# A fused stack of four graph layers: probabilities of the second graph turned through DRAM and VectorE

## What is computed

```python
# layer 0: attention with 4 heads
Wh = (x @ W).reshape(B, N, H, F)
e = leaky_relu(e_src[:, :, None, :] + e_dst[:, None, :, :], 0.2)
alpha = softmax(where(adj > 0, e, NEG_INF), axis=2)
x = layernorm(x + elu(einsum('bijh,bjhf->bihf', alpha, Wh)))
# layer 1: three rounds of neighbour sum and GRU cell
for i in range(3):
    aggr = einsum('bst,bsd->btd', adj != 0, h @ weight[i])
    h = gru_cell(aggr, h)
x = layernorm(x + h)
# layer 2: per relation r = 1..4 of adj == r, sum and weight; adj holds 0 and 1 here
x = layernorm(x + sum_r (adj == r) @ x @ weight[r] + bias)
# layer 3: attention with one head
x = layernorm(x + elu(softmax(where(adj > 0, e3, NEG_INF)) @ (x @ W3.T)))
```

## Time and profile before

| what | us |
|---|---|
| median of 3 runs | 2617.78 (2617.44 to 2618.26) |
| span of the profiled execution | 2616.2 |
| TensorE busy in it | 2564.6 (98%) |
| VectorE busy | 2064.6 (79%) |
| ScalarE busy | 1629.9 (62%) |
| GpSimd busy | 1093.8 (42%) |
| mean granted TensorE clock | 0.992 of full |

### The profile page before, as it was taken

One profiled execution on the slowest core, in us unless ns is written; L12 is line 12 of the kernel. 1 busy time (PEld: TensorE's weight loads), 2 busy tenths in 40 slices (PEclk: granted clock), 3 DMA queues, 4 the chain that ended last, 5 costly groups with the idle time before them and its releaser, 6 DMA issues.

```text
span 2616.2 us, 48544 instructions
## 1 busy us (share of the span) xinstructions
PE 2564.6 (98%) x14979; PEld 2219.6 (85%) x14979; DVE 2064.6 (79%) x5210; ACT 1629.9 (62%) x4153; POOL 1093.8 (42%) x1264
## 2 busy tenths in 40 slices
...
DMA packets 265105, 128.99 MB, mean 49 GB/s; under 512 B 139760, under 2 KB 249840, under 8 KB 264816
## 3 DMA queue, kind: packets, MB, share of 16 engines
...
## 4 chain that ended last, share of the span: by engine, by line
PE 94%; DVE 1%; issue 1%; ACT 0%; POOL 0%; POOLq 0%; DVEq 0%; ACTq 0%
PE psum L938 60%; PE psum L792 10%; PE psum L926 6%; PE psum L853 6%; PE psum L975 3%; PE psum L842 3%; PE psum L869 2%; PE psum L811 1%; PE psum L913 1%; PE psum L861 1%; DVE stats L1351 0%; ACT x L1176 0%; POOL rstd L1508 0%; DVE first_scores L1322 0%; DVE moments L1355 0%
## 5 line engine op out<-in xcount | busy, mean ns | idle before, releaser
L938 PE MATMUL psum<-ag_h,wc_h 128*128 128x512 f32 (+1 forms) x1188 | 489.0, 412 | 2.7 <-issue 2.0
L938 PE MATMUL psum<-ht_h,whh_h 128*128 128x512 f32 (+1 forms) x1188 | 483.0, 407 | 0.7 <-ACT g_z L1159 0.6
L938 PE MATMUL psum<-ht_h,whh_l 128*128 128x512 f32 (+1 forms) x1188 | 462.8, 390 | 0.0
L938 PE MATMUL psum<-ag_l,wc_h 128*128 128x512 f32 (+1 forms) x1188 | 461.9, 389 | 0.0
L938 PE MATMUL psum<-ht_l,whh_h 128*128 128x512 f32 (+1 forms) x1188 | 461.7, 389 | 0.0
L938 PE MATMUL psum<-ag_h,wc_l 128*128 128x512 f32 (+1 forms) x1188 | 461.5, 388 | 0.0
L1506 POOL TENSOR_SCALAR rstd<-moments 128x2 f32<-128x2 f32 x256 | 73.3, 286 | 858.6 <-DVE moments L1355 854.1
L1557 POOL TENSOR_TENSOR ht<-ht,g_n 128x512 f32<-128x512 f32 (+1 forms) x198 | 251.7, 1271 | 71.3 <-ACT g_n L1164 63.7
L938 PEld LDWEIGHTS psum<-ht_h,whh_l 128*128 128x128 f32 x1188 | 224.9, 189 | 50.8
L938 PEld LDWEIGHTS psum<-ag_h,wc_l 128*128 128x128 f32 x1188 | 223.4, 188 | 50.5
L938 PEld LDWEIGHTS psum<-ht_l,whh_h 128*128 128x128 f32 x1188 | 225.7, 190 | 40.0
...
## 6 DMA issues: line engine op xcount, KB each, us to landing
first_scores<-first_kept SPq DMA_DIRECT2D x116, 256.0 KB, 3.7
adj_i<-in_adj_dram SPq DMA_DIRECT2D x128, 128.0 KB, 3.2
x_in<-in_x_dram SPq DMA_DIRECT2D x64, 256.0 KB, 3.8
out_dram<-out_t ACTq DMA_DIRECT2D x64, 256.0 KB, 2.5
x_blocks<-in_x_dram SPq DMA_DIRECT2D x464, 32.0 KB, 2.1
part<-in_adj_dram SPq DMA_DIRECT2D x32, 256.0 KB, 3.3
adj_g<-in_adj_dram SPq DMA_DIRECT2D x31, 256.0 KB, 3.3
last_scores<-last_kept SPq DMA_DIRECT2D x59, 128.0 KB, 3.0
```

What stands on the lines that cost most here:

```text
L938: last = mm(dst, s, m, start=(first and k == 0), stop=(last_part and k == len(flat) - 1))
```

## The change

For units from 6 on and the second graph of the unit (`scratched`), TensorE's four transposes and VectorE's copy go. In their place SP stores the unit's four probability tiles (256 KB) to a DRAM scratch (`pt_keep`), after ScalarE has made all eight, and loads them again in 32x32 pieces (`pt_blocks`, four DMAs of 64 KB) into a tile of the ring `xs`, and VectorE turns this with one block transpose of 128x512 into `first_turned`. The ring `xs` has three tiles instead of two, `wh` three. `x_blocks` is issued as four DMAs instead of eight. The scores tile of the second graph is free when it is stored. `att_pt(pre,1,0,1)` (now VectorE alone), `att_pv(pre,1,0)` and `att_exp(pre,1,0)` stand later in `HALF`. The weights of relations 2 to 4 aren't loaded at the start in one 768 KB tile, but one by one into a tile of 256 KB, by SP inside a branch like that of the other engines; SP reads the flag for it (`learn`).

```diff
-SLOTS = {"light": 4, "adj": 2, "x": 2, "xt": 1, "wh": 2,
+SLOTS = {"light": 4, "adj": 2, "x": 2, "xt": 1, "wh": 3,
...
-         "post_pen": 2, "post_t": 1, "post_pt": 1, "post_hn": 1, "post_y": 1, "x2s": 1, "h1": 1, "mt": 1, "adjt": 2, "x3": 2, "xs": 2,
+         "post_pen": 2, "post_t": 1, "post_pt": 1, "post_hn": 1, "post_y": 1, "x2s": 1, "h1": 1, "mt": 1, "adjt": 2, "x3": 2, "xs": 3,
...
+def scratched(kind, u, q):
+
+    return kind == "pre" and u >= BLOCKED and q == 1
...
+    if name == "att_pt" and not scratched(*a):
+        out.append("light")
...
-gru_r(0,0,0)  att_prob(pre,1,0)  rel_adjt(-2,1)
-gru_z(0,0,0)
+gru_r(0,0,0)  att_prob(pre,1,0)  pt_keep(1,0)  rel_adjt(-2,1)
+gru_z(0,0,0)  pt_blocks(1,0)
 gru_in(0,0,0)
-gru_hn(0,0,1)  att_pt(pre,1,0,0)  att_wh(post,-2,0,0)  gru_new(-1,1,1)  gru_split(-1,1)  att_pt(pre,1,0,1)
+gru_hn(0,0,1)  att_pt(pre,1,0,0)  att_wh(post,-2,0,0)  gru_new(-1,1,1)  gru_split(-1,1)
         att_wh(post,-2,0,1)  att_rows(post,-2,0)  att_spread(post,-2,0,0)  att_xt(pre,1,1)  rel_mask(-2,1)  gru_n(0,0,0)
-gru_rzh(0,0,1)  gru_turn(-1,1,0)  att_pv(pre,1,0)  gru_new(0,0,0)  att_wh(pre,1,1,0)  att_wh(pre,1,1,1)  att_rows(pre,1,1)
-        rel_h1(-2,1)  att_exp(pre,1,0)  gru_turn(-1,1,1)
+gru_rzh(0,0,1)  gru_turn(-1,1,0)  gru_new(0,0,0)  att_wh(pre,1,1,0)  att_wh(pre,1,1,1)  att_rows(pre,1,1)
+        rel_h1(-2,1)  gru_turn(-1,1,1)
 gru_r(0,0,1)  att_norm(post,-3,1)  rel_y1(-2,1)  att_spread(pre,1,1,0)  att_scores(post,-2,0,0)
-gru_z(0,0,1)  rel_rest(-2,1)
-gru_in(0,0,1)
+gru_z(0,0,1)  rel_rest(-2,1)  att_pt(pre,1,0,1)
+gru_in(0,0,1)  att_pv(pre,1,0)  att_exp(pre,1,0)
 gru_agg(-1,2,0)  att_prob(post,-2,0)  att_res(pre,1,0)  att_store(post,-3,1)  gru_n(0,0,1)  rel_norm(-2,1)
 gru_agg(-1,2,1)
 gru_hn(-1,2,0)  att_pt(post,-2,0,0)
 gru_rzh(-1,2,0)  att_xt(post,-2,1)  gru_new(0,0,1)  gru_split(0,0)  att_pv(post,-2,0)  att_spread(pre,1,1,1)
         att_scores(pre,1,1,0)  att_scores(pre,1,1,1)
 gru_r(-1,2,0)
-gru_z(-1,2,0)  att_wh(post,-2,1,0)  att_wh(post,-2,1,1)  att_exp(post,-2,0)  att_prob(pre,1,1)  x_blocks(2,0)  pre_load(2,0)
+gru_z(-1,2,0)  att_wh(post,-2,1,0)  att_wh(post,-2,1,1)  att_exp(post,-2,0)  att_prob(pre,1,1)  pt_keep(1,1)  x_blocks(2,0)  pre_load(2,0)
         gru_n(-1,2,0)
-gru_in(-1,2,0)
...
-        wrs = sb("wrs", [P, R - 1, C, D])
+        wr_other = sb("wr_other", [P, C, D])
...
+        pt_kept = [nc.dram_tensor(f"pt_kept{i}", (P, H0, P), F32, kind="Internal").ap() for i in range(2)]
...
+        TURNED = [s for s in order if s[0] == "att_xt" and blocked(*s[1:]) or s[0] == "att_pt" and scratched(*s[1:])]
...
+        def turned_on_pe(kind, u, q):
+
+            return min(u, BLOCKED) + u + q + 1 if kind == "pre" else u + 1
...
+                    (kind + "_t", "att_spread"): (s_pt_kept, 16 * (u - BLOCKED + 1)) if scratched(kind, u, q) else (L.pt_psum, turned_on_pe(kind, u, q)), (kind + "_pt", "att_pt"): (L.pv_psum, u + 1),
...
+            def pt_keep(u):
+                L = LAY["pre"]
+                sp.wait_ge(L.prob, 2 * L.heads * (u + 1))
+                if scratched("pre", u - 2, 1):
+                    sp.wait_ge(L.pt_ready, 2 * u - 2)
+                sp.dma_start(pt_kept[u % 2], L.scores[scores_slot("pre", u, 1)][:]).then_inc(s_pt_kept, 16)
+
+            def pt_blocks(u):
+                i = take(sp, "xs", "pt_blocks", u)
+                sp.wait_ge(s_pt_kept, 16 * (u - BLOCKED + 1))
+                blocks = pt_kept[u % 2].rearrange("(b i) h (a j) -> a i h b j", i=TURN, j=TURN)
+                for a in range(P // TURN):
+                    sp.dma_start(xs[i][a * TURN:(a + 1) * TURN].rearrange("i c n -> i (c n)").rearrange("i (h b j) -> i h b j", h=H0, j=TURN),
+                                 blocks[a]).then_inc(s_xs[i], 16)
+
             def x_blocks(u):
                 i = take(sp, "xs", "x_blocks", u)
-                blocks = x[2 * u:2 * u + 2].rearrange("g (b i) (c f j) -> c f i g b j", i=TURN, f=P // TURN, j=TURN)
-                for c in range(C):
-                    for g in range(P // TURN):
-                        sp.dma_start(xs[i][g * TURN:(g + 1) * TURN, c, :], blocks[c, g].rearrange("i g b j -> i (g b) j")).then_inc(s_xs[i], 16)
+                blocks = x[2 * u:2 * u + 2].rearrange("g (b i) (c f j) -> f i c g b j", i=TURN, f=P // TURN, j=TURN)
+                for f in range(P // TURN):
+                    sp.dma_start(xs[i][f * TURN:(f + 1) * TURN].rearrange("i c (m j) -> i c m j", j=TURN),
+                                 blocks[f].rearrange("i c g b j -> i c (g b) j")).then_inc(s_xs[i], 16)
 
             def gru_load(k):
...
-                sp.dma_start(wrs[:], L2_gnn_weight[1:R].rearrange("r (c p) o -> p r c o", p=P)).then_inc(s_rest, 16)
...
+            def rel_rest(u):
+
+                with sp.If(any_other > 0):
+                    for r in range(2, R + 1):
+                        after(sp, s_yr_ps, (R - 1) * u + r - 2)
+                        sp.dma_start(wr_other[:], L2_gnn_weight[r - 1].rearrange("(c p) o -> p c o", p=P)).then_inc(s_wr, 16)
+
...
+                if scratched(kind, u, q):
+                    return
...
-                if u == 0:
-                    pe.wait_ge(s_rest, 48)
...
+                        pe.wait_ge(s_wr, 16 * n)
...
-                                last = mm(LIGHT[:, i, q * D:(q + 1) * D], hr_t[:, c, q * P:(q + 1) * P], wrs[:, r - 2, c, :],
+                                last = mm(LIGHT[:, i, q * D:(q + 1) * D], hr_t[:, c, q * P:(q + 1) * P], wr_other[:, c, :],
...
-                    dve.wait_ge(s_xs[i], 128 * (rounds + 1))
+                    dve.wait_ge(s_xs[i], 64 * (rounds + 1))
...
-                L, i = LAY[kind], slot("light", "att_pt", kind, u, q)
+                L = LAY[kind]
                 pi = take(dve, kind + "_pt", "att_pt", kind, u, q)
-
                 dve.wait_ge(L.pt_ready, 2 * u + 1)
-                dve.wait_ge(L.pt_psum, 2 * u + q + 1)
-                nc.vector.tensor_copy(L.turned[pi][:].rearrange("p h n -> p (h n)"), LIGHT[:, i, :]).then_inc(L.pt_ready, 1)
+                turned = L.turned[pi][:].rearrange("p h n -> p (h n)")
+                if scratched(kind, u, q):
+                    i, rounds = ring("xs", "pt_blocks", u)
+                    dve.wait_ge(s_xs[i], 64 * (rounds + 1))
+                    nc.vector.transpose(turned, xs[i][:].rearrange("p c n -> p (c n)")).then_inc(s_xturned, 1)
+                    dve.wait_ge(s_xturned, TURNED.index(("att_pt", kind, u, q)) + 1)
+                    dve.sem_inc(L.pt_ready, 1)
+                else:
+                    i = slot("light", "att_pt", kind, u, q)
+                    dve.wait_ge(L.pt_psum, 2 * u + q + 1)
+                    nc.vector.tensor_copy(turned, LIGHT[:, i, :]).then_inc(L.pt_ready, 1)
```

More of the change, by code:

```diff
@@ L41 @@
     "pre_load": ("adj", "x", "pre_pen"), "post_load": ("adj", "post_pen", "adjf"),
-    "att_xt": ("xt",), "x_blocks": ("xs",), "att_direct": ("light",),
-    "att_pt": ("light",), "att_pv": ("light",),
+    "att_xt": ("xt",), "x_blocks": ("xs",), "pt_blocks": ("xs",), "att_direct": ("light",),
+    "att_pv": ("light",),
     "rel_adjt": ("light", "adjt"), "rel_bias": ("x2s",), "rel_mask": ("mt",),
@@ L108 @@
 gru_r(-1,2,0)
-gru_z(-1,2,0)  att_wh(post,-2,1,0)  att_wh(post,-2,1,1)  att_exp(post,-2,0)  att_prob(pre,1,1)  x_blocks(2,0)  pre_load(2,0)
+gru_z(-1,2,0)  att_wh(post,-2,1,0)  att_wh(post,-2,1,1)  att_exp(post,-2,0)  att_prob(pre,1,1)  pt_keep(1,1)  x_blocks(2,0)  pre_load(2,0)
         gru_n(-1,2,0)
-gru_in(-1,2,0)
+gru_in(-1,2,0)  pt_blocks(1,1)
 gru_hn(-1,2,1)  gru_turn(0,0,0)  gru_turn(0,0,1)  gru_load(1)
@@ L291, in placed @@
         return []
+    if name in ("pt_keep", "pt_blocks") and not scratched("pre", u, 1):
+        return []
     return [(name,) + kind + (u,) + a[2:]] if 0 <= u < 2 * halves - 2 else []
```

30 lines of the change are left out of this document (19 added, 11 removed).

## The result

The changed kernel takes 2973.99 us (median of 4 runs, 2971.48 to 2976.74) against 2618.02 us for the kernel before on the same chip: 1.136 times as long, interval 1.134 to 1.138. That is 356 us, or 12.3 us in each of the 29 rounds, where 8.6 were forecast. The time lies 4 us above the top of the range.

The account below looks back on a forecast made before the run. TensorE's matmul time was taken to set the span. Even unit 5.7, odd unit 1.7 and clock 1.2 made 8.6 us per round, x 29 = 249 us, giving 2867 us (+9.5%), range 2735 to 2970.

Parts of the forecast that it names:

- the chain at the even unit: Store waits for probabilities, adj_i queues behind it, GpSimd waits for adj_i, VectorE for GpSimd, TensorE for VectorE; 5.7 us net.
- the forecast signs: Changed kernel's profile: TensorE busy near 2539 us, 89%; waits near 2 and 6 us, 29 each; late adj_i; clock below 1.
- The even wait: TensorE at att_pv of the even unit waits 6.1 us for the turned tile; net of the saving +3.3 to +7.7.
- "by pieces" bound of 4.3: SP's four x block loads at the even unit take 4.3 us to issue if time goes by pieces; 2.7 was taken.
- The odd wait: TensorE waits 1.7 us at the odd unit, as VectorE's turn now stands behind the relation layer's statistics.
- 0.4 us added for SP's loads: Odd unit: SP's block loads ahead of the last layer's score rows may delay scores and VectorE; between 0 and 2.1 us.
- The saving: Four transposes per unit leave TensorE's stream, 0.44 us per unit, 25.5 us over 58 units.
- the term for the clock: TensorE's granted clock falls after a long wait, slowing the work behind it; 1.2 us per round, bounds 0 to 3.4.
- The third: Both units wait, block loads go by pieces, 6.8 us at low clock follows each wait; 2966 to 3039 us; chance 0.06.
- The second: Only the odd unit waits, slack absorbs the late even update; 2655 us; chance 0.08 with other partial waits.
- The fourth: Reloaded probabilities are themselves the late input, up to 2 us more per round, 2925 us; counted within the forecast's 0.80.
- The first: Everything is hidden, the engines keep ahead and only the 25.5 us go; 2592 us, faster; chance 0.04.

Follow-up runs that it names:

- e2_odd_turn: Changed kernel, but VectorE turns the odd unit's block right after rel_h1 instead of behind the relation layer's statistics; 2851.9 us, ratio 1.089.
- e3_filler: Changed kernel, with matmuls of unused result ahead of TensorE's waits for the turned tile, 7 at the odd unit, 20 at the even; 2841.86 us, ratio 1.086.
- e7_adj_first: Changed kernel, but at the even unit SP issues adj_i and x_in of the next unit ahead of the probability store; 2847.41 us, ratio 1.088.
- e1_sp_order: Changed kernel, but at the even unit SP stores and reloads the probabilities only after the next unit's loads are issued; 2749.27 us, ratio 1.048.
- the mended version: Changed kernel with SP's next loads first, odd turn right after rel_h1, even turned tile used after gru_hn(0,1,0); 2607.92 us, 0.997 of the kernel before.

## Why the prediction was off

**What was right.** The sign, the two places, and each link of the chain at the even unit. Of the forecast signs, these showed: TensorE's share 91% (89% expected), waits in two sizes 27 times each in 27 rounds, GpSimd waiting for adj_i, VectorE for GpSimd, a clock below 1. One did not: TensorE's busy time was to fall to 2539 us and rose to 2716.0, and the share came out near only because the span grew too. The assumption on which all rested, that the other engines do not catch up, held: TensorE asked for the even tile 1376.55 - 1369.56 = 7.0 us after the probabilities were complete, and 6.85 was used.

**The even wait** was taken as 6.1 us and is 4.8 in the round shown (5.0 on average). The issue times were good: the four block loads took 2.70 us, exactly what was taken, so they go mostly by instruction and the "by pieces" bound of 4.3 is out. What was too long are the parts behind: GpSimd had adj_i 2.6 us after its issue and not 3.4, and its two operations took 1.08 + 1.26 us where 1.36 + 1.42 were copied from single instances of before. All of it shortens one chain, from 13.0 to 1381.34 - 1369.56 = 11.8 us.

**The odd wait** was taken as 1.7 us and is 1.67, by the working with VectorE's list. The 0.4 us added for SP's loads was not needed. `e2_odd_turn` shows that it was VectorE's order and not a DMA.

**The saving** was 0.88 us per round and is 0.66. The 0.44 us for four transposes came from half of a block of eight; the other four still stand there, and what surrounds them still costs a change of shape. Why the difference is just that large stays open.

**The step that failed is the term for the clock**: "I take 1.2, with 0 to 3.4 as bounds." It is 5.9 us per round by the account of busy time, and at least 4.6 by `e3_filler`, outside its own bounds either way. The 1.2 also does not price the prediction's own sentence that "each long wait is paid for again in the work behind it". Two things were wrong in it. I priced one low stretch per round, behind the even wait, while the odd wait of 1.7 us is followed by one as well; the upper bound of 3.4 holds only one stretch too. And between "inside the wait" (zero) and "on work" (half of it) I took a point near zero, with no row for it, although the only row at hand, the idle 2.48 us of the earlier trace rows, has about 6 of its 6.8 us on work. From the earlier trace rows alone, two waits with 3.4 to 6.8 us each would have given 3.4 to 6.8 us per round; with 1.7 + 6.1 of waits that is 10.3 to 13.7 net, 2917 to 3015 us. The time missed the range by only 4 us because the other terms erred the opposite way: waits of 6.1 + 1.7 + 0.4 = 8.2 us were forecast and idle time grew by 7.1, which hid 1.1 of the 4.7 us by which the clock was too low.

**The rivals.** The third gave 2966 to 3039 us and holds the time, but by luck. Its blocks by pieces did not happen. And its 12 to 14.5 us contain one stretch of 6.8 us per round, although its words say one behind each wait; priced by its words it is 7.7 + 1.7 + 6.8 = 16.2 us, 3088 us. What it had right is that both waits are followed by low clock. The second, absorbed by slack, is out: the even wait is there in every round. The fourth showed only where the order was changed (2.2 us per round in `e7_adj_first`, 1.2 in `e1_sp_order`); as the kernel stands, VectorE never waits for the reload. The first is refuted for the kernel as it stands, and the mended version shows what it is worth: at most 10 us, not 25. The rule of the Trainium skill, "TensorE: Matmul & The Clock Gate", section "Part 1: The HAM clock gate (the "warmup" mystery)", that activity releases the throttle, agrees with `e3_filler`: matmuls without use in place of the waits, and the clock is back at 1.00.
